# One-hot comparisons of a codebook lookup, written with an accumulator output

## The reference

```
x = layernorm(x + attention(x, wq, wk, wv, wo))      # 32 heads, rotary, causal
Wg = codebook[idx_gate].reshape(2752, 1024)          # codebook: 16384 entries of 8 numbers
Wu = codebook[idx_up].reshape(2752, 1024)
Wd = codebook[idx_down].reshape(1024, 2752)
x = layernorm(x + (silu(x @ Wg.T) * (x @ Wu.T)) @ Wd.T)
```

## Time and profile before

| | us |
|---|---|
| median of 3 runs | 7436.8 |
| lowest and highest run | 7423.39, 7446.76 |
| the profiled execution | 7463.33 |
| its span, first to last instruction | 7461.5 |

### The profile page before, as it was taken

How to read it: one execution, slowest core, us unless ns; L and a number is a source line. 1 busy time by engine, 2 the same in 40 slices (tenths; PEclk the granted TensorE clock), 3 DMA queues, 4 the chain that set the end, 5 groups by cost and what they waited for, 6 DMA issues and landing times.

```text
span 7461.5 us, 100268 instructions
## 1 busy us (share of the span) xinstructions
PE 6801.4 (91%) x29072; PEld 4369.7 (59%) x29072; DVE 5099.5 (68%) x10313; ACT 900.0 (12%) x2076; POOL 5617.9 (75%) x5316
## 2 busy tenths in 40 slices
PE   8999999999999999999999999999999999683426
PEld 3444666664676566666666666666666666452313
DVE  3321777772799888888888888888888888472303
ACT  0001777771000000000000000000000000000001
POOL 7777777777898777777777777777777777777774
PEclk9999999999999999999999999999999999887768
DMA  4232111121333233323333323223332333221101
GB/s 123 65 82 43 35 32 33 32 56 35 76 90 84 62 72 71 69 66 71 70 70 72 73 67 70 70 71 71 70 71 64 71 71 70 38 63 37 26 12 47
DMA packets 472304, 460.97 MB, mean 62 GB/s; under 512 B 231120, under 2 KB 347728, under 8 KB 467536
## 3 DMA queue, kind: packets, MB, share of 16 engines
q10 hardware_dynamic: 287072, 396.73, 18.8%
q0 software_dynamic: 169984, 22.10, 7.4%
q1 hardware_dynamic: 14832, 36.84, 1.3%
HBM read 398.07 MB, written 57.15 MB: 61 GB/s over the span
## 4 chain that ended last, share of the span: by engine, by line
POOL 75%; issue 24%; PE 1%; DVE 0%; ACT 0%; DMA 0%; POOLq 0%; DVEq 0%; ACTq 0%
POOL raw L196 75%; PE ps L452 0%; PE ps L526 0%; DVE small L988 0%; ACT arena L799 0%; DMA out_dram<-arena 0%; DMA raw<-in_codebook_dram,idx_sb 0%; PE ps L519 0%; DMA idx_sb<-in_idx_dram 0%; POOLq L204 0%; DVE small L991 0%; POOLq L70 0%; POOLq L194 0%; DVE small L998 0%; ACT arena L706 0%
## 5 line engine op out<-in xcount | busy, mean ns | idle before, releaser
L196 POOL DMA_INDIRECT raw<-in_codebook_dram,idx_sb x5312 | 5617.7, 1058 | 1764.6 <-issue 1761.5
L406 PE MATMUL ps<-onehot,table 128*128 128x512 f32 x11776 | 3066.5, 412 | 254.0 <-DVE picked L945 248.8
L937 DVE TENSOR_SCALAR onehot<-arena,small 128x512 fp32r<-128x512 f32 x5896 | 2657.2, 504 | 907.5 <-PE ps L406 679.9
L406 PEld LDWEIGHTS ps<-onehot,table 128*128 128x128 f32 x11776 | 2214.2, 189 | 1016.5 <-issue 320.2
L434 PE MATMUL ps<-big,arena 128*128 128x512 f32 (+1 forms) x2816 | 1284.2, 593 | 228.6 <-DVE arena L922 227.3
L945 DVE SCALAR_TENSOR_TENSOR picked<-arena,small,ps 128x512 fp32r<-128x512 f16 x1472 | 1026.9, 737 | 0.0
L434 PEld LDWEIGHTS ps<-big,arena 128*128 128x128 f32 (+1 forms) x2816 | 525.2, 187 | 743.4 <-issue 478.8
L851 DVE TENSOR_REDUCE small<-ps 128x1 f32<-128x384 f32 (+7 forms) x512 | 374.1, 752 | 437.3 <-PE ps L299 437.3
L452 PE MATMUL ps<-arena 128*128 128x512 f32 (+1 forms) x1408 | 647.7, 596 | 2.0 <-ACT arena L706 1.1
L930 DVE TENSOR_TENSOR big<-ps,big 128x512 f32<-128x512 f32 x704 | 471.7, 686 | 93.3 <-PE ps L452 88.8
L417 PE MATMUL ps<-picked,sel 128*128 128x512 f32 x1472 | 470.8, 401 | 9.6
(11 more groups left out here) (66 smaller groups left out, 2473.4 us busy)
## 6 DMA issues: line engine op xcount, KB each, us to landing
arena<-code_low ACTq DMA_DIRECT2D x738, 256.0 KB
arena<-code_high ACTq DMA_DIRECT2D x738, 128.0 KB
raw<-in_codebook_dram,idx_sb POOLq DMA_INDIRECT x5312
gathered_units<-raw SPq DMA_DIRECT2D x40, 512.0 KB, 2.8
arena<-gathered_units ACTq DMA_DIRECT2D x20, 1024.0 KB
queries_keys<-arena ACTq DMA_DIRECT2D x16, 1024.0 KB, 4.0
arena<-queries_keys ACTq DMA_DIRECT2D x32, 512.0 KB
big<-in_xT_dram ACTq DMA_DIRECT2D x4, 2048.0 KB, 17.3
```

Source lines behind the costliest of these rows:

```text
L196: pool.indirect_dma_start(raw[:, s, n, :], None, codebook, bass.IndirectOffsetOnAxis(ap=idx_sb[:, s, n:n + 1], axis=0),).then_inc(gathered ...
L406: last = mm(ps[:, bank + c, :], table[:, k, c, :], onehot[:, k, :], start=(k == 0), stop=(k == KLO - 1))
L937: dve.tensor_scalar(onehot[:, k, :], lo_sb[:, s % 2, :], kp_sb[:, k:k + 1], None, ALU.is_equal).then_inc(onehot_ready, 1)
```

## The change

The comparison gets a second operation, an addition, and an accumulator output: besides the 512 ones and zeros it now sums them per partition and writes the sum to one column of `small`. Column k of `hits` takes the sum of part k; nobody reads it. `hits` lies on columns 34 to 41, which are free by then. The main output is the same as before. All comparisons are changed, in the 96 slots and in the passes, and all stay on VectorE.

```diff
+        hits = small[:, 34:42]
...
                 past(dve, onehot_used, first * KLO + ((s - 1) * KLO + k + 1))
+
                 dve.tensor_scalar(onehot[:, k, :], lo_sb[:, s % 2, :], kp_sb[:, k:k + 1], None,
-                                  ALU.is_equal).then_inc(onehot_ready, 1)
+                                  ALU.is_equal, ALU.add, accum_out=hits[:, k:k + 1]).then_inc(onehot_ready, 1)
```

## The result

The changed kernel takes 7840.3 us (median of 4 runs, 7836.1 to 7845.2) where the one before takes 7441.8 (4 runs): ratio 1.0536, interval 1.0507 to 1.0564. The profiled execution has a span of 7834.1 us.

A forecast was written before the change was run, and what follows sets the result against it. GpSimd's gathers bound the kernel, lookups close behind; slower comparisons make lookups the bound: 1936.4 + 6.0 + 699.8 (first slots) + 5470 (passes) + 54 (turns) + 221 (tail) = 8387 us, scaled to 8360, range 7890 to 8830.

The forecast's parts named there:

- The pace: VectorE's comparisons: accumulating form streams one element a cycle, not two, adding 0.270 us each, 2.16 us per eight.
- The read: Writing out the sum after each VectorE comparison: 0.08 us each, 0.64 per eight, bounds 0 and 0.16.
- the bound of 0: Lower bound of the read, hidden in the overlap of back-to-back instructions: sum 7916 us, 7890 once scaled.
- The loop turn: At 19 turns of the loop over passes, comparisons start another 2.83 us late, 54 us in all.
- Additions: In 11 slots of a pass, VectorE's additions make pick to comparisons 3.23 us, the slot 9.21 us.
- First slots, closed chain, start and tail: 96 first slots of 7.29 us; pass slots, comparisons waiting on TensorE and back, 8.20; lookups from 1936.4; tail 221 us.
- The gathers: GpSimd freed by the form: 5312 gathers at the attention's rate take 6850 us, their path ending at about 6930.
- The range: Kernel time between 7890 and 8830 us, from a read of 0 to one of 0.16 us.
- the rivals: Two-element pace kept, 7523 us, 0.06; cheap form freeing GpSimd, 7065 us, 0.03; TensorE's clock falling, 8550 us, 0.07.
- rival 3: TensorE's clock falls, as it waits in each slot, busy some 80% in passes: 8550 us, chance 0.07.

The follow-up runs named there:

- e7: Kernel before, comparisons without accumulator reading 495 of 512 columns as 15 runs of 33 with gaps; 14,282.0 us, a single run on the second kind of chip.
- e2: Kernel before with the accumulating form in the first 96 slots alone; 13,773.3 us against 13,563.4 on the second kind of chip, ratio 1.0154.
- e4: Kernel before with two of eight comparisons accumulating, in first slots and pass slots not behind additions; 13,617.0 us against 13,563.4, ratio 1.0040.
- e1: Kernel before with all comparisons as an operation on two inputs, no accumulator; 14,106.0 us, ratio 1.0400, on the second kind of chip.
- e2b: Kernel before with the accumulating form in the first 96 slots alone, where gathers and lookups run together; 7180.5 us against 7425.5, ratio 0.9666.
- e11: Kernel before plus 768 comparisons on spare memory beside running gathers, 256 each of old form, accumulating, two inputs; one gather took 96.00 us.

## Why the prediction was wrong

It was right on the direction, on the lost pace as a cause and on the chain; it took the loss more than twice too large. Its steps, one by one:

- **The pace**, one element a cycle for two: 2.16 us per eight forecast, 5.33 - 3.18 = 2.15 measured; e7 has the same pace without the accumulator. Right.
- **The read: this step failed.** The Trainium skill (VectorE: DVE Perf Modes, Two Vector instructions with no wait between them) says that such an operation is two instructions. The trace agrees, with a row of 82 ns for each read, but the read starts together with the next instruction and adds some 0.013 us at most by e7, and nothing that the timeline shows. The prediction drew from the page that the bound of 0 would not be reached, which the page doesn't state and the trace refutes. I had taken 0.08 per comparison, from a row on VectorE whose follower depended on nothing either, and from ScalarE's 0.09. 8 x 0.08 x 737 = 472 of the 553 us by which the sum (8387) exceeds the span (7834). The lower bound, read at 0, is what the traces show; I gave it no weight because two rows spoke for a price, and neither was this instruction.
- **The loop turn**, 19 x 2.83 us. I carried it over from the earlier trace rows as a fixed cost. In the changed kernel the comparisons behind a turn start 3.12 to 3.51 us after the pick (below a turn with 3.33), where 3.12 is usual for a slot with additions: 1.7 us for all the 18 turns between two passes, so some 52 of the 54 us were too many. In e2, e4 and before, whose passes go at TensorE's pace, it is 5.7 to 6.8. Being behind with its work isn't all that VectorE needs for that: in e1 and e7 it sets the pace of the passes too, with the same chain, and the comparisons behind a turn start 4.5 to 5.5 us (pitch 0.602) and 3.4 to 4.6 us (pitch 0.636) after the pick. The slower the comparisons, the less a turn costs; that the queue reads ahead over the branch, and further the more work lies in front of it, is argued, not tested.

```profile
3585.78 1.39 DVE L947 SCALAR_TENSOR_TENSOR picked<-arena,small,ps 128x512 fp32r<-128x512 f16 x2
3587.10 1.87 DVE L931 TENSOR_TENSOR big<-ps,big 128x512 f32<-128x512 f32 x3
...
3589.11 0.74 DVE L939 TENSOR_SCALAR_CACHE_REDUCE onehot<-arena,small 128x512 fp32r<-128x512 f32 x1
```

- **Additions**: pick to comparisons is 3.12 us when the products are all waiting, and not the 3.23 of a slot in which VectorE waited for one: 0.11 x 220 = 24 us.
- **First slots, closed chain, start and tail**: 6.65 us against 6.65 (read at 0), 7.57 against 7.56, lookups from 1930.9 and not 1936.4, 215 us of tail and not 221. Right within 11 us together. The read, the turns, the additions and these come to 472 + 52 + 24 + 11 = 559 us, for the 553 by which the sum is too large.
- **The gathers** at the attention's rate: the last one at 6821.7, forecast about 6850. Right, and worth nothing in the changed kernel, as said; e2b shows the 245 us that it is worth where the lookups leave room. Of the kernel before the prediction names the two waits of the tail alone; the two in the passes, 223.1 us, are missing, but no term of the sum hangs on them.
- **The range** ended at a read of 0, which was itself 7890. The turn and the additions, both taken as fixed, had no bounds of their own; with them at what the changed kernel shows, 52 and 24 us less, the lower end would have been some 7815.

Of the rivals, none came: the clock stayed at 0.996 in the mean. TensorE waited for the pick in nearly every slot of the passes, 538.7 us over 635 waits with a median of 0.60, and was busy for 195.73 of 217 us, 90% and not the 80% of rival 3.

## What to carry to other kernels

When two engines share a port, price a slower form twice: by what it adds on its own engine and by what it gives the other one, and use it only where the second path sets the end. Here it is worth 3.3% in the first 96 slots and costs 5.4% everywhere, on the kind of chip where gathers and lookups run together; on the other kind the first 96 slots alone cost 1.5%. A follow-up instruction that shows as a row need not cost its queue anything; only the distance between starts tells. And a bubble read from a place where an engine waits is not a fixed cost: here it went from 2.83 us to a tenth of a microsecond on the mean when the engine got more work.

## What the runs showed of the hardware beyond that

- An unbroken run of 253 comparisons in the two-element form held a single gather for 96.00 us; one slower comparison in a run of eight raised the gathers from 49 to 128 in 187 us.
- The pitch of a 128x512 comparison in float32 is 0.396 us in the two-element form, 0.602 on two inputs and 0.667 with an accumulator. With 1.053 ns a column, for 256 columns in the first form and 512 in the others, the fixed parts are an estimated 0.13, 0.06 and 0.13 us.
- On one kind of chip the same program takes 13,563 us for 7430. Beside running gathers each VectorE instruction came 1.40 us after the last one in e11, reads counted, with no wait for another engine that the trace shows; the two lines below are of e11. In e1 TensorE's granted clock was 0.50, the lower level, from 200 to 7400 us, while the gathers ran and TensorE was busy for 1762 of these 7200 us, and 0.99 behind them. What makes these chips differ stays open.

```profile
251.85 0.74 DVE L834 TENSOR_SCALAR_CACHE_REDUCE arena<-arena,small 128x512 f32<-128x512 f32 x1 [1.30 <-DVE arena L834]
253.26 0.08 DVE L834 DVE_READ_ACCUMULATOR arena<-arena,small 128x1 f32 x1 [0.67 <-issue]
```
